# Routing into the first expert: which groups of slots, gathers and weights come ahead of it

## The reference

```python
gate = jax.nn.softmax(tok @ Wgate.T, axis=-1)
k_cap = bs // E                                   # 4096 // 8 = 512
vals, idx = jax.lax.top_k(gate.T, k_cap)
idx_flat = idx.T.reshape(-1)
w = vals.T
g = _ln(tok[idx_flat], mlp_g, mlp_b).reshape(k_cap, E, d)
y = jnp.einsum('ked,ehd->keh', g, fc1s) + b1s     # 256 -> 1024
y = jax.nn.gelu(y, approximate=True)
y = jnp.einsum('keh,edh->ked', y, fc2s) + b2s     # 1024 -> 256
y = y * w[..., None]
tok = tok.at[idx_flat].add(y.reshape(-1, d))
```

## Time and profile before

| | us |
|---|---|
| median of 3 runs | 2855.84 |
| lowest and highest run | 2855.83, 2857.46 |
| span of the profiled execution | 2859.8 |
| TensorE busy in it | 2583.2 |
| VectorE, ScalarE, GpSimd busy in it | 1614.8, 1050.9, 486.5 |

### The profile page before, as it was taken

The page is one execution under the profiler, slowest core; times in us unless marked ns, Lnnn a source line. Parts: engine busy times, 40 slices in busy tenths (PEclk is TensorE's granted clock), DMA queues, the critical chain, the costliest instruction groups (busy, mean ns, idle before and its releaser), DMA issues.

```text
span 2859.8 us, 60211 instructions
## 1 busy us (share of the span) xinstructions
PE 2583.2 (90%) x24161; PEld 1815.8 (63%) x24161; DVE 1614.8 (56%) x3691; ACT 1050.9 (37%) x2104; POOL 486.5 (17%) x407
## 2 busy tenths in 40 slices
PE   6888599999999946997999999997998888799999
PEld 5666366666666644665888888884444677556555
DVE  6999778787878773122455555443333677722221
ACT  4555365555555501211333333332121666411110
POOL 2223110101010103332111111110000656400000
PEclk9999899999999957998999999998998999999999
DMA  5000000000000032434100000000000233200000
GB/s 203 2 2 2 12 23 22 29 22 29 22 29 22 19 97 95 129 104 112 48 0 0 0 0 0 0 1 1 0 0 0 86 95 97 60 8 15 7 15 15
DMA packets 72121, 101.90 MB, mean 36 GB/s; under 512 B 10864, under 2 KB 50288, under 8 KB 71472
## 3 DMA queue, kind: packets, MB, share of 16 engines
q1 hardware_dynamic: 65840, 91.46, 10.0%
q0 software_dynamic: 6144, 8.56, 1.5%
HBM read 67.20 MB, written 32.80 MB: 35 GB/s over the span
## 4 chain that ended last, share of the span: by engine, by line
PE 79%; DVE 13%; issue 3%; ACT 2%; DMA 1%; POOL 1%; another core or an unknown queue 0%; SPq 0%; DVEq 0%; ACTq 0%
PE psW L320 16%; PE psW L313 8%; PE psS L1322 7%; PE psP L435 4%; PE psP L1288 4%; PE psP L428 4%; PE psP L1282 4%; PE psS L1316 4%; PE psO L1282 4%; PE psO L1288 4%; PE psS L379 3%; PE psO L412 3%; PE psO L344 2%; PE psW L528 2%; PE psP L395 2%
## 5 line engine op out<-in xcount | busy, mean ns | idle before, releaser
L320 PE MATMUL psW<-r,work 128*128 128x512 f32 x1024 | 481.6, 604 | 1.0 <-DVE work L755 1.0
L1218 POOL TENSOR_TENSOR work<-work 128x512 f32<-128x512 f32 x128 | 132.1, 1043 | 1141.8 <-DVE work L777 1141.7
L320 PEld LDWEIGHTS psW<-r,work 128*128 128x128 f32 x1024 | 180.6, 191 | 162.4 <-issue 156.8
L313 PE MATMUL psW<-work,r 128*128 128x128 f32 x2048 | 244.2, 278 | 1.0 <-DVE work L755 1.0
L313 PEld LDWEIGHTS psW<-work,r 128*128 128x128 f32 x2048 | 235.6, 193 | 3.5 <-DVE work L755 1.4
L766 DVE TENSOR_REDUCE work<-psS 128x8 f32<-128x512 f32 x256 | 175.4, 685 | 92.6 <-PE psS L558 55.8
L1322 PE MATMUL psS<-r,work 128*128 128x256 f32 x960 | 211.2, 381 | 5.3 <-DVE work L1385 5.3
L1322 PEld LDWEIGHTS psS<-r,work 128*128 128x128 f32 x960 | 181.2, 190 | 32.8 <-DVE work L1385 6.1
L768 DVE TENSOR_TENSOR work<-psS,work 128x512 f32<-128x512 f32 x256 | 176.9, 691 | 11.3
L1138 ACT ACTIVATE work<-work 128x512 f32<-128x512 f32 x128 | 80.1, 626 | 276.4 <-DVE work L768 276.4
L1196 POOL TENSOR_TENSOR work<-work,head_mask 128x1024 f32<-128x1024 f32 x64 | 121.2, 1894 | 207.0 <-ACT work L1074 204.5
(11 more groups left out here) (271 smaller groups left out, 4656.7 us busy)
## 6 DMA issues: line engine op xcount, KB each, us to landing
r<-in_l_fc SPq DMA_DIRECT2D x16, 1024.0 KB
rotated<-work SPq DMA_DIRECT2D x60, 256.0 KB
work<-mod_rows SPq DMA_DIRECT2D x64, 128.0 KB, 2.8
work<-rotated SPq DMA_DIRECT2D x30, 256.0 KB
r<-in_l_w SPq DMA_DIRECT2D x2, 3072.0 KB, 19.2
x<-in_x SPq DMA_DIRECT2D x8, 512.0 KB, 9.2
gather_table<-work SPq DMA_DIRECT2D x32, 128.0 KB, 1.8
moe_sum<-work SPq DMA_DIRECT2D x32, 128.0 KB, 1.7
```

The costliest lines, as they stand in the source:

```text
L313: ins = nc.tensor.matmul(ps[:, q * P:(q + 1) * P], w[:, k, lo + q * P:lo + (q + 1) * P], L.hT[:, k, :], start=(k == 0), stop=(k == KC - 1))
L320: ins = nc.tensor.matmul(ps[:, 0:width], L.hT[:, k, :], w[:, k, lo:lo + width], start=(k == 0), stop=(k == KC - 1))
L1218: nc.gpsimd.tensor_tensor(E, E, halves(L.rs)[i].unsqueeze(2).broadcast_to([P, 8, N]), ALU.mult).then_inc(L.s[f"prob{i}"].sem, 1)
```

## The change

It moves work on all five engines; no arithmetic is added or taken away.

- **VectorE:** only the tables of groups 0 and 1 are built in the routing. Those of groups 2 and 3 are built in expert 0's step, behind its modulation and ahead of the normalisation of expert 1's tokens.
- **GpSimd:** product of group 0, gather 0, product of group 1, gather 1, products of groups 2 and 3.
- **TensorE:** sums and turns of groups 0 and 1 in the routing; the wait for all groups in front of the experts goes. In step 0 it waits for two groups ahead of the hidden matmuls, sums groups 2 and 3 behind them, turns them behind expert 1's transposes, and waits for all four groups ahead of the result, since groups 2 and 3 now use the banks psS.
- **ScalarE:** copies and slot writes of groups 2 and 3 stand behind expert 0's GELUs.
- **SyncE:** expert 1's weights come ahead of the wait for the third group's sums, and layer 2's two weights behind it.

Of the diff, what only renames or moves text is kept short:

```diff
@@ in pe_ff @@
             def step(t, u, half, ahead):
+                late_slots = Q.kind == "moe" and is_first(t)
+                if late_slots:
+                    pe.wait_ge(rt["slots"], 2)
                 hidden(t, u, half)
+                if late_slots:
+                    for i in range(2, len(GROUPS)):
+                        pe_slot_sums(pe, i)
                 if ahead:
                     turn(t + 1)
+                if late_slots:
+                    for i in range(2, len(GROUPS)):
+                        pe_slot_turn(pe, i)
+                    pe.wait_ge(rt["slots"], len(GROUPS))
                 result(t, u)
@@ in dve_ff @@
             def step(t, u, half, ahead):
                 ch.reset()
+                if Q.kind == "moe" and is_first(t):
+                    for i in range(2, len(GROUPS)):
+                        dve_hot_a(i)
+                        dve_hot_b(i)
                 if ahead:
                     norm(t + 1, 1 - u, half + u)
@@ in act_ff, behind the loop over the GELUs @@
+                if Q.kind == "moe" and is_first(t):
+                    for i in range(2, len(GROUPS)):
+                        act_slots(a, i)
@@ in pool_moe @@
-            for i in range(3):
-                pool_hot(g, i)
+            pool_hot(g, 0)
             g.wait_ge(st["tab"], 32 * NT)
             g.wait_ge(st["gates"], 16)
             gather(0)
-            pool_hot(g, 3)
+            pool_hot(g, 1)
             gather(1)
+            for i in range(2, len(GROUPS)):
+                pool_hot(g, i)
@@ in sp_moe @@
                 if ahead:
                     sp_expert(sp, Q, t + 1, 1 - u)
+                if is_first(t):
+                    sp.wait_ge(rt["ix"], 3)
+                    for dst, name in ((l2_w1, "l2_w1"), (l2_w2, "l2_w2")):
+                        sp.dma_start(dst, A[name].rearrange("(k p) n -> p k n", p=P)).then_inc(ld["l2"], 16)
@@ in dve_route @@
-            dve_hot_a(0)
-            dve_hot_b(0)
-            for i in range(1, len(GROUPS)):
+            for i in range(2):
                 dve_hot_a(i)
-            for i in range(1, len(GROUPS)):
                 dve_hot_b(i)
@@ in pe_route; pe_slot_sums and pe_slot_turn hold what stood in its loop @@
-            for i, (lo, hi) in enumerate(GROUPS):
...
+            for i in range(2):
+                pe_slot_sums(pe, i)
+                pe_slot_turn(pe, i)
+
+        SLOT_SUMS = [psP[:, 0:512], psP[:, 512:1024], psS[:, 0:256], psS[:, 512:768]]
+        SLOT_TURNS = [psO[:, 0:512], psO[:, 512:1024], psS[:, 256:512], psS[:, 768:1024]]
@@ SyncE, ahead of the experts @@
             sp.wait_ge(su["mm2"], 2)
-            sp.wait_ge(rt["ix"], 3)
-            for dst, name in ((l2_w1, "l2_w1"), (l2_w2, "l2_w2")):
-                sp.dma_start(dst, chunked(name)).then_inc(ld["l2"], 16)
             sp.wait_ge(st["tab"], 32 * NT)
@@ TensorE @@
             pe_route(pe)
-            following(pe, "route")
             pe_ff(pe, Q["moe"])
```

More of the change, by code:

```diff
@@ L1258, in is_last_expert, with is_first @@
             return Q.kind == "moe" and isinstance(t, int) and t == NG - 1
+        def is_first(t):
+            return isinstance(t, int) and t == 0
         HB = [psP[:, 0:512], psP[:, 512:1024], psO[:, 0:512], psO[:, 512:1024]]
@@ L1862, in pe_route, with pe_slot_sums, pe_slot_turn @@
             ins.then_inc(rt["back"], 1)
-            for i, (lo, hi) in enumerate(GROUPS):
-                n, bank = hi - lo, i % 2 * 512
-                _, numbered, second = hots[i]
-                pe.wait_ge(rt["hoti"], i + 1)
-                pe.wait_ge(rt["hotb"], i + 1)
-                for t in range(NT):
-                    ins = nc.tensor.matmul(psP[0:16 * n, bank:bank + 32 * n], numbered[:, t, :], second[:, t, :],
-                                           start=(t == 0), stop=(t == NT - 1))
-                ins.then_inc(rt["ix"], 1)
-                pe.wait_ge(rt["ixc"], i + 1)
-                for e in range(n):
-                    for q in range(4):
-                        ins = nc.tensor.matmul(psO[32 * q:32 * q + 32, bank + 4 * e:bank + 4 * e + 4],
-                                               slot_rows[:, lo + e, :], ident[:, 16 * e + 4 * q:16 * e + 4 * q + 4],
-                                               start=True, stop=True)
-                ins.then_inc(rt["turn"], 1)
+            for i in range(2):
[3 more added lines that the diff above has]
+        SLOT_TURNS = [psO[:, 0:512], psO[:, 512:1024], psS[:, 256:512], psS[:, 768:1024]]
+        def pe_slot_sums(pe, i):
+            lo, hi = GROUPS[i]
+            n = hi - lo
+            _, numbered, second = hots[i]
+            pe.wait_ge(rt["hoti"], i + 1)
+            pe.wait_ge(rt["hotb"], i + 1)
+            for t in range(NT):
+                ins = nc.tensor.matmul(SLOT_SUMS[i][0:16 * n, 0:32 * n], numbered[:, t, :], second[:, t, :],
+                                       start=(t == 0), stop=(t == NT - 1))
+            ins.then_inc(rt["ix"], 1)
+        def pe_slot_turn(pe, i):
+            lo, hi = GROUPS[i]
+            pe.wait_ge(rt["ixc"], i + 1)
+            for e in range(hi - lo):
+                for q in range(4):
+                    ins = nc.tensor.matmul(SLOT_TURNS[i][32 * q:32 * q + 32, 4 * e:4 * e + 4],
+                                           slot_rows[:, lo + e, :], ident[:, 16 * e + 4 * q:16 * e + 4 * q + 4],
+                                           start=True, stop=True)
+            ins.then_inc(rt["turn"], 1)
         def act_route(a):
@@ L1883, in act_route, with act_slots @@
             nc.scalar.activation(gates[:, :, 0:E8], probs, ACT.Copy).then_inc(rt["gates"], 1)
[L1884 to L1892 removed]
+            for i in range(2):
+                act_slots(a, i)
+        def act_slots(a, i):
+            lo, hi = GROUPS[i]
+            n = hi - lo
+            a.wait_ge(rt["ix"], i + 1)
+            nc.scalar.activation(slot_rows[0:16 * n, lo:hi, :],
+                                 SLOT_SUMS[i][0:16 * n, 0:32 * n].rearrange("p (e s) -> p e s", s=32), ACT.Copy
+                                 ).then_inc(rt["ixc"], 1)
+            a.wait_ge(rt["turn"], i + 1)
+            nc.scalar.activation(slots[:, lo:hi, :], SLOT_TURNS[i][:, 0:4 * n].rearrange("p (e r) -> p e r", r=4),
+                                 ACT.Identity, bias=middle[:, 0:1]).then_inc(rt["slots"], 1)
         L = [Attention(i) for i in range(4)]
```

8 lines of the change are left out of this document (removed).

## The result

The changed kernel takes 2848.84 us (median of 7 runs, 2844.28 to 2854.70) against 2857.46 us (7 runs, 2855.83 to 2859.12). The ratio is 0.9971, with a 95% interval of 0.9960 to 0.9981: 8.6 us less by the medians, where 14.3 were forecast. The predicted 2841.5 is 7 us low, and the time lies at the upper end of the range.

The account below looks back on a forecast made before the run. TensorE, busy 2583.2 of 2859.8 us, was taken as the bound, gains lying only where it waits. Terms −18.8 + 2.5 + 1.95 = −14.3 us gave a span of 2845.5, less 4.0 a time of 2841.5; range 2838 to 2849.

Parts of the forecast that it names:

- Gather 0: GpSimd: expert 0's gather issues start at 1073.6, behind group 0's slots, and end at 1079.8.
- Landing and tokens: Gathers land 2.2 us behind their last issue; VectorE normalises expert 0's tokens from 1082.0 to 1084.0.
- Product 1 and the transposes: Group 1's product on GpSimd, 1080.0 to 1081.9, and its chain free TensorE for expert 0's transposes at 1084.5.
- Hidden matmuls: TensorE, expert 0: they start at 1088.2, 3.7 us behind the transposes' start, and last 15.6 us.
- Sums of groups 2 and 3: TensorE, between expert 0's hidden matmuls and expert 1's transposes: 2.5 us added (2.3 to 4.6) at full clock.
- The turns: TensorE and ScalarE behind expert 1's transposes: turns and wait for all slots expose about 1.95 us before the result matmuls.
- Work in time: VectorE's tables and tokens, GpSimd's gather 1 and products stay hidden in expert 0's step; worst corner costs 1 to 2.
- The rival of a clock falling behind the hidden matmuls: Clock falls at the end of expert 0's step: about +3.5 us, 2845, at worst 2850; chance 0.20.
- 18.8 us earlier: Start of expert 0's hidden matmuls on TensorE: 1088.2 instead of 1107.00, the main gain.
- pure waiting for groups that expert 0 doesn't need: TensorE's wait for all slot groups before expert 0's transposes, 1095.95 to 1103.29: 7.3 us.
- the 4.0 us that the prediction took off the span: Profiled span less median of runs shown (2855.84), subtracted from the forecast span of 2845.5 to give 2841.5.
- The rival on this stall: ScalarE's unexplained 7.1 us comes back at expert 0's slot writes or GELUs: 2848.6; chance 0.10.

Follow-up runs that it names:

- b_again: The kernel before, without an edit, profiled and timed again on the chip of comparison 1: 2863.80 us, ratio 1.0006 to before beside it.
- e_quiet: The kernel before with SyncE's part alone (expert 1's weights without the wait, layer 2's later): 2860.74 us against 2863.01, ratio 0.9991.
- e_gather: The kernel before with GpSimd's order alone changed (product 0, gather 0, product 1, gather 1, products 2 and 3): 2863.03 us against 2856.45, ratio 1.0019.
- a_fourth: The changed kernel, without a further edit, profiled and timed a fourth time: 2848.86 us against 2857.11 for before beside it, ratio 0.9965.
- e_quiet2: The kernel before with SyncE's part alone, once more on another chip: 2857.45 us against 2857.11 for before, ratio 0.9999.
- e_l2_first: The changed kernel with SyncE's order of before (layer 2's weights ahead of expert 1's): 2849.82 us against 2856.45 for before, ratio 0.9974.

## Why the prediction was right about the mechanism and wrong about the size

Its steps, in their order. Places are again from the first table, 1068.72 in the profile that the prediction used.

- **Gather 0.** Issues from 4.9 to 11.1 forecast, 5.7 to 10.8 measured. GpSimd took 0.96 us instead of 0.2 from the slot write to its first issue (0.27 at gather 1), and the issues were shorter, since VectorE's tables were (2.28 for that of 2048, not 3.10). The first one took 1.37 and ended 1.0 behind the table beside it, as I had taken it.
- **Landing and tokens.** 13.3 forecast, 12.7 measured; landing 1.9 against 2.2.
- **Product 1 and the transposes.** 15.8 forecast, 15.3 measured, and set by group 1's chain as said (the tokens were done 0.8 earlier).
- **Hidden matmuls.** 19.5 forecast, 19.1 measured in all four profiles of the changed kernel.
- **Sums of groups 2 and 3.** 2.5 forecast, 2.5 measured (1111.04 to 1113.54). The turns and the wait: 1.95 forecast, 1.6 measured.
- **Work in time.** No wait of TensorE on it. GpSimd's last two products took 3.1 and 5.8 us, together above the 4.6 to 7.8 forecast, and ended 5 us before they were wanted; expert 1's tokens were normalised at 1108.5, transposed from 1113.5.
- **A term that was missing.** The hidden matmuls took 16.6 to 16.7 us instead of 15.6 in three of four profiles of the changed kernel, because the granted clock rose 5.4 to 5.7 us behind their start and not 3.5. The rival of a clock falling behind the hidden matmuls did not happen (granted 1.00 through sums, turns and result); what varied was its rise at their start.

So the path of the changed kernel was right to 0.5 us up to the hidden matmuls, and its stretch to 0.8 (1776.8 forecast, 1777.6 measured). **The step that failed is the other end of the subtraction**, "18.8 us earlier" than 38.3. The 38.3 contain the wait that the prediction put down as "pure waiting for groups that expert 0 doesn't need", 7.3 us. It is in the profiled execution and, 1 to 3 us shorter, in b_again and e_quiet on one chip. In the two profiles of the kernel before from other chips the hidden matmuls start at 31.4 and 32.4, and 12.3 and 13.3 us are to be had. With about 4.1 for sums and turns 8.2 and 9.2 remain at the first result matmul and 8.8 and 9.7 in the stretch, and 8.3 and 7.9 were timed. That the timed runs of the first result had no late turn either is argued from their level, 2857.5; no trace of them was kept.

The second wrong term is the 4.0 us that the prediction took off the span as a constant. In all seventeen later profiles the timed execution is 1.8 to 2.4 us longer than its span (2854.70 and 2852.8 for the changed kernel). So the profiled execution of before would have taken 2861.6 to 2862.2 us, about 6 more than the median that the prediction had and more than any of the seven timed runs: it was another execution than those, with an idle time of 7.1 us and no releaser in its middle. The rival on this stall asked whether it would come back in the changed kernel. It should have asked whether the timed runs had it at all. The distance alone proves nothing, though: the changed kernel's profiled run also lies 5.9 us above its median, and there it is the seam of layers 0 and 1 that took longer.

The rule of the Trainium skill (SBUF — State Buffer, "Who interferes with whom"), by which two-input operations of VectorE are inferred not to hold the descriptors of GpSimd's DMAs, is not borne out here. Issues that began beside such operations took 1.14 to 2.99 us in the changed kernel, e_gather and before, and 0.95 with VectorE idle. Several ended 0.8 to 1.0 us behind the end of such an operation: in e_gather the first (1079.99, the table 1078.97) and the fourth (1087.46, the table 1086.64).

## What to carry to other kernels

A subtraction has two ends, and the profile of the kernel before is one execution. Before a wait in it counts as gain, compare its length with how far the profiled execution lies above the timed ones, and take a second profile of the kernel before, on another chip if there is one: a wait without a releaser may be absent from the timed runs. And of edits that belong together each may be worth nothing or less alone: here the early gather costs 0.2% by itself, the order of the weights gives nothing with or without the rest, and the early gather with TensorE's shorter wait makes 0.3 to 0.4%.

## What the runs showed of the hardware that was not expected

- The same program, before, took 2863.0 us on one chip and 2856.5 to 2857.3 on three others, while the changed kernel stayed at 2848.8 to 2850.9. What goes with it in the profiles is that work which TensorE had finished was seen late: its last turn 4.3 us (e_quiet) and 5.7 us (b_again) behind the recorded end of its matmuls on that chip, and 7.1 us in the first profile, and the last sums 0.8 to 0.9 us. In the same profiles the second group's slots also were 0.3 us later (15.3 against 15.0).
- The granted clock comes back at different moments of the same work. Behind 19.10 us of routing it came back 3.3 us behind the start of the hidden matmuls in a_fourth and 5.7 behind it in the first profile. At half clock and then at full, by stretch:

```profile
1094.00:1100.00 6.00, 5.69 (x7) 2.52 (x8) 6.00 (x4) 1.84 (x2) 4.98 (x3) 0.50 0.26 71
1100.00:1111.00 11.00, 11.00 (x26) 4.57 (x24) 8.43 (x7) 4.25 (x7) 8.94 (x5) 1.00 0.09 25
```

```profile
1088.50:1091.50 3.00, 2.99 (x4) 1.45 (x5) 3.00 (x2) 0.00 (x0) 2.67 (x3) 0.50 0.44 116
1091.70:1105.00 13.30, 13.30 (x61) 6.10 (x59) 10.93 (x8) 6.68 (x9) 10.68 (x5) 1.00 0.08 21
```

  The first pair is the changed kernel's first profile, the second a_fourth. The first result matmul comes at 39.8 and 41.0 us, 1.2 apart with no edit between them, and an earlier start of the matmuls can be given back in part by a longer time at half clock (0.5 of 1.1 us in e_quiet2).
- The start of the first table lay between 1068.7 and 1075.9 us in eighteen profiles. It goes with the clock at the seam of layers 0 and 1: where that averaged 0.65 between 308 and 372 us (the changed kernel's first profile and e_l2_first) the first table starts at 1075.2 and 1075.9, and where it averaged 0.79 (six profiles) at 1068.7 to 1069.7.
